# The next chunk's context in four whole rows, loaded into the place of its low part

## What is computed

```python
# x [1,64,512], ctx [1,6272,512]; 32 query heads on 8 key/value heads of 128
q = (layernorm(x) @ Wq + bq)            # 32 heads
k, v = split(ctx @ Wkv + bkv)           # 8 heads each
scores = einsum(q, k) / sqrt(128)
attn = softmax(scores)                  # over all 6272 keys
x = x + (attn @ v) @ Wo + bo
# then: weights are table[codes] * scales (4-bit codes), LoRA parts are added
x = x + attn_and_ffn(layernorm(x))
x = x + linear_with_fourier_update(layernorm(x))
```

## Time and profile before

| | us |
|---|---|
| median of 3 runs | 1094.21 |
| lowest and highest | 1093.18, 1095.26 |
| the profiled execution | 1092.23 |
| its span, first to last instruction | 1090.4 |
| busy in it: PE, DVE, ACT, POOL | 1048.7, 761.8, 586.8, 471.9 |
| idle of PE ahead of `p_kv` matmuls that waited for `v_lo` | 8.5 |
| idle of ACT ahead of `ctx_hi`, waiting for the load of `ctx_st` | 15.5 and 14.5 |
| idle of POOL ahead of `ctx_lo`, waiting for ACT | 25.2 and 24.9 |

### The profile page before, as it was taken

One profiled execution on the slowest core, in us unless ns is written; L12 is line 12 of the kernel. 1 busy time (PEld: TensorE's weight loads), 2 busy tenths in 40 slices (PEclk: granted clock), 3 DMA queues, 4 the chain that ended last, 5 costly groups with the idle time before them and its releaser, 6 DMA issues.

```text
span 1090.4 us, 19501 instructions
## 1 busy us (share of the span) xinstructions
PE 1048.7 (96%) x7035; PEld 959.6 (88%) x7035; DVE 761.8 (70%) x1651; ACT 586.8 (54%) x1233; POOL 471.9 (43%) x633
## 2 busy tenths in 40 slices
PE   6989999999999999999999999999999997999786
PEld 4989999999999999999999999999999996998332
DVE  3447777787777877767877778777777764776663
ACT  2136565566555665556665556655566553665210
POOL 2025454454445454445543454544555433443320
PEclk9689999999999999999999999999999998999988
DMA  9612222122212221121211222212212126435574
GB/s 354 237 48 66 57 66 68 47 75 64 65 53 67 61 66 56 55 70 57 78 63 45 66 71 62 66 39 70 72 57 75 40 63 208 127 112 153 160 233 138
DMA packets 68340, 98.96 MB, mean 91 GB/s; under 512 B 7636, under 2 KB 36820, under 8 KB 67604
## 3 DMA queue, kind: packets, MB, share of 16 engines
q1 hardware_dynamic: 66884, 90.33, 26.9%
q10 hardware_dynamic: 1120, 6.03, 1.4%
q0 software_dynamic: 240, 1.36, 0.3%
HBM read 82.79 MB, written 14.89 MB: 90 GB/s over the span
## 4 chain that ended last, share of the span: by engine, by line
PE 85%; DVE 3%; DMA 2%; SPq 2%; POOL 1%; issue 1%; ACT 0%; POOLq 0%; DVEq 0%
PE p_kv L73 18%; PE p_kv L74 18%; PE p_kv L75 18%; PE p_t L721 8%; PE p_o L73 4%; PE p_o L74 4%; PE p_o L75 4%; PE p_s L774 2%; PE p_s L73 2%; PE p_s L74 2%; PE p_s L75 2%; SPq L511 2%; DMA expanded_weights<-slots 1%; PE p_ot L709 1%; DMA ring_lo<-expanded_weights 1%; DVE probs L1162 1%
## 5 line engine op out<-in xcount | busy, mean ns | idle before, releaser
L603 POOL TENSOR_SCALAR slots<-code 128x512 f32<-128x512 bf16 x232 | 154.2, 665 | 240.3 <-DVE slots L1178 159.0
L1174 DVE TENSOR_TENSOR slots<-slots 128x512 f32<-128x512 f32 x232 | 175.6, 757 | 10.4 <-POOL slots L603 8.4
L1030 ACT ACTIVATE slots<-code,drop_and_offsets 128x512 f32<-128x512 bf16 x232 | 148.4, 714 | 30.7 <-POOL slots L623 30.7
L623 POOL TENSOR_TENSOR slots<-slots 128x512 f32<-128x512 f32 x58 | 75.8, 1307 | 195.9 <-DVE slots L1174 195.9
L1127 DVE TENSOR_TENSOR v_lo<-p_kv,v_hi 128x256 fp32r<-128x256 f32 x196 | 83.1, 424 | 109.2 <-ACT v_hi L997 108.0
L997 ACT ACTIVATE v_hi<-p_kv 128x256 fp32r<-128x256 f32 x196 | 75.2, 384 | 148.2 <-PE p_kv L75 148.0
L997 ACT ACTIVATE k_hi<-p_kv,bk_sb 128x448 fp32r<-128x448 f32 x112 | 71.1, 635 | 154.2 <-PE p_kv L75 153.9
L1129 DVE SCALAR_TENSOR_TENSOR k_lo<-p_kv,bk_sb,k_hi 128x448 fp32r<-128x448 f32 x112 | 76.4, 682 | 108.6 <-ACT k_hi L997 107.6
L1139 DVE TENSOR_TENSOR pt_lo<-p_t,pt_hi 128x512 fp32r<-128x512 f32 x224 | 133.5, 616 | 23.2 <-ACT pt_hi L1008 23.1
L1008 ACT ACTIVATE pt_hi<-p_t 128x512 fp32r<-128x512 f32 x224 | 115.2, 543 | 38.9 <-PE p_t L721 38.9
L73 PE MATMUL p_kv<-wkv_hi,ctx_even_hi 128*128 128x256 f32 x448 | 127.1, 284 | 8.6 <-DVE v_lo L1127 7.7
(11 more groups left out here) (208 smaller groups left out, 2742.7 us busy)
## 6 DMA issues: line engine op xcount, KB each, us to landing
code<-in_codes SPq DMA_DIRECT2D x58, 256.0 KB, 2.6
scale<-in_scales SPq DMA_DIRECT2D x116, 128.0 KB, 3.1
expanded_weights<-slots SPq DMA_DIRECT2D x56, 256.0 KB, 2.0
ctx_st<-in_ctx_t SPq DMA_DIRECT2D x96, 112.0 KB, 2.1
wq_sb<-in_wq SPq DMA_DIRECT2D x8, 1024.0 KB, 13.8
ring_hi<-expanded_weights SPq DMA_DIRECT2D x22, 256.0 KB, 5.5
ring_lo<-expanded_weights SPq DMA_DIRECT2D x22, 256.0 KB, 5.7
stage<-in_wkv ACTq DMA_DIRECT2D x4, 1024.0 KB, 8.6
```

The source lines that it names most:

```text
L603: nc.gpsimd.tensor_scalar(slots[:, slot, :], code16[:], LINES[j][0], LINES[j][1], ALU.mult, ALU.add).then_inc(pool_lines, 1)
L1030: nc.scalar.activation(slots[:, slot, :], code16[:], ACT.Identity, bias=offsets[:, k:k + 1], scale=LINES[j][0]).then_inc(act_lines, 1)
L1174: nc.vector.tensor_tensor(slots[:, slot, :], slots[:, slot, :], slots[:, other, :], ALU.max).then_inc(merged, 1)
```

## The change

The staging place goes. A load now brings one whole row of the next chunk, 128x896, straight to the place of its low part (`ctx_raw` is a second name for `ctx_even_lo` and `ctx_odd_lo`). ScalarE rounds the whole row from there into the high part, and GpSimd subtracts in place: the raw row is overwritten with the low part. So there are four loads, four roundings and four subtractions for a chunk instead of sixteen of each. Loads no longer wait for a subtraction; from the third chunk on, a load waits for the last use of the place by TensorE two chunks earlier. Each row has a semaphore of its own. The rows are spread over the pairs by `PAIR_PIECES = (2, 1, 1, 0)`: two in pair 0, one each in pairs 1 and 2, always the first one in the even block behind value tile 1, and in pair 0 the second one behind the second turned probabilities. A place of the same size as the old staging place stays reserved for the small tensors that lie over it in the later parts.

```diff
--- before.py
+++ after.py
@@ -61,9 +61,8 @@
 GU_TILES = KT * GU_COLS
 NT = ATT_TILES + GU_TILES + FT
 EXTRA = NT - NCH * NKV
-PIECE = CHUNK // 4
-PIECES = KT * (CHUNK // PIECE)
-PAIR_PIECES = (5, 5, 5, 1)
+PIECES = KT
+PAIR_PIECES = (2, 1, 1, 0)
 EPS = 1e-5
 HIGHEST = 3.0e38
 
@@ -307,7 +306,7 @@
 
 
     with ExitStack() as st:
-        ctx_st = sb(st, "ctx_st", [P, PIECE], F32)
+        sb(st, "small_rows", [P, 224], F32)
         ctx_hi = [even_hi, sb(st, "ctx_odd_hi", [P, KT, CHUNK], F32R)]
         ctx_lo = [even_lo, sb(st, "ctx_odd_lo", [P, KT, CHUNK], F32R)]
         v_hi = sb(st, "v_hi", [P, CT, 2 * D], F32R)
@@ -333,7 +332,8 @@
         p_o = psum(st, "p_o", [P, 512])
         p_ot = psum(st, "p_ot", [P, 512])
 
-        ctx_in, ctx_rounded, ctx_split = sem("ctx_in"), sem("ctx_rounded"), sem("ctx_split")
+        ctx_in = [sem(f"ctx_in{k}") for k in range(KT)]
+        ctx_rounded, ctx_split = sem("ctx_rounded"), sem("ctx_split")
         kv_psum, kv_rounded, kv_split = sem("kv_psum"), sem("kv_rounded"), sem("kv_split")
         scores_psum, scores_out = sem("scores_psum"), sem("scores_out")
         stat_step, max_ready = sem("stat_step"), sem("max_ready")
@@ -388,6 +388,7 @@
 
             return nc.alloc_sbuf_tensor_at(name, shape, F32, offset=where[place] + skip)
 
+        ctx_raw = [over("ctx_even_raw", [P, KT, CHUNK], "ctx_even_lo"), over("ctx_odd_raw", [P, KT, CHUNK], "ctx_odd_lo")]
         ring_odd = over("ring_odd", [P, RING_ODD, 2, TW], "ctx_odd_hi")
         extra = over("extra_tiles", [P, EXTRA, TW], "ctx_odd_hi", RING_ODD * 2 * TW * 4)
         ring_hi = over("ring_hi", [P, KT, 2 * NKV * D], "wkv_hi")
@@ -416,7 +417,7 @@
         bb_sb, lb_d, w_four, z2t = place_in_turn("probs", (
             ("bb_sb", row), ("lb_d", [RANK, HID]), ("w_four", [RR, HID]), ("z2t", turned_rows)))
         e_small, = place_in_turn("o_t", (("e_small", [RANK, 4, TOK]),))
-        stats, mv, spare = place_in_turn("ctx_st", (
+        stats, mv, spare = place_in_turn("small_rows", (
             ("stats", [TOK, 2, 6]), ("mv", [TOK, 2, 4]), ("spare", [P, 8])))
 
         pb = [p_kv[:, 0], p_kv[:, 1], p_s[:, 0], p_s[:, 1], p_t[:, 0], p_t[:, 1], p_o[:], p_ot[:]]
@@ -480,10 +481,9 @@
         def _(sp):
             def load_ctx(s, piece, first=False):
 
-                if not first:
-                    sp.wait_ge(ctx_split, PIECES * (s - 1) + piece)
-                k, q = piece // 4, piece % 4
-                sp.dma_start(ctx_st[:], ctx_t[s, k, :, q * PIECE:(q + 1) * PIECE]).then_inc(ctx_in, 16)
+                if s >= 2:
+                    sp.wait_ge(kv_psum, k_use(s - 2, NKV - 2, 1) + 1)
+                sp.dma_start(ctx_raw[s % 2][:, piece], ctx_t[s, piece]).then_inc(ctx_in[piece], 16)
 
             def codes_of(n, first=False):
                 if not first:
@@ -585,11 +585,9 @@
         def _(pool):
             def split_ctx(s, piece, half):
 
-                n, k = PIECES * (s - 1) + piece, piece // 4
-                keys = slice(piece % 4 * PIECE, (piece % 4 + 1) * PIECE)
-                wait_apart(pool, ctx_rounded, n + 1, pool_passed)
-                nc.gpsimd.tensor_tensor(ctx_lo[half][:, k, keys], ctx_st[:], ctx_hi[half][:, k, keys].bitcast(F32),
-                                        ALU.subtract).then_inc(ctx_split, 1)
+                wait_apart(pool, ctx_rounded, PIECES * (s - 1) + piece + 1, pool_passed)
+                nc.gpsimd.tensor_tensor(ctx_lo[half][:, piece], ctx_raw[half][:, piece],
+                                        ctx_hi[half][:, piece].bitcast(F32), ALU.subtract).then_inc(ctx_split, 1)
 
             def narrow(n, first=False):
                 wait_apart(pool, code_in, 16 * (n + 1), pool_passed)
@@ -1017,9 +1015,9 @@
                 if last or q >= PAIR_PIECES[h // 2]:
                     return
                 piece = sum(PAIR_PIECES[:h // 2]) + q
-                act.wait_ge(ctx_in, 16 * (PIECES * s + piece + 1))
-                keys = slice(piece % 4 * PIECE, (piece % 4 + 1) * PIECE)
-                nc.scalar.activation(ctx_hi[1 - par][:, piece // 4, keys], ctx_st[:], ACT.Copy).then_inc(ctx_rounded, 1)
+                act.wait_ge(ctx_in[piece], 16 * (s + 1))
+                nc.scalar.activation(ctx_hi[1 - par][:, piece], ctx_raw[1 - par][:, piece], ACT.Copy).then_inc(
+                    ctx_rounded, 1)
 
             def lines(n, first=False):
```

## The result

The changed kernel takes 1113.52 us (median of 4 runs, 1111.93 to 1115.45) against 1093.7 for the kernel before (4 runs, 1093.09 to 1095.26). The ratio is 1.0172, with a 95% interval of 1.0138 to 1.0207: slower by 19.8 us, where 18.3 was forecast (1112.5, range 1102 to 1122). The profiled execution of the changed kernel is the slowest of its four, 1115.45, with a span of 1113.5.

What follows compares the result with a forecast made beforehand. TensorE was taken as the bound, so what counts is whether `v_lo` comes in time. Late tiles -1.5 and 18 places x 1.1 = 19.8 sum to +18.3 us on the median 1094.2: 1112.5 us, range 1102 to 1122.

Steps and rivals of the forecast that it cites:

- Late tiles: Two value tiles start late on TensorE behind a late GpSimd subtraction; loads no longer wait for it: -1.5 us.
- Step 1, the load: Even blocks, 18 places: row load issued at 238.0, lands 3.3 us later, up to 4 allowed; 4.2 still costs nothing.
- the prediction's own sign: Load or rounding is wrong if ScalarE waits for the row by more than about 0.5 us.
- The rival of the late row: Row lands 4.7 us after issue instead of 4.2, sliding rounding and subtraction by 0.5: 9 us more, 1121.5; chance 0.10.
- Step 2, the rounding: ScalarE between value tiles 1 and 2: 0.94 us in 0.93 free, no cost if the row landed.
- Step 3, the subtraction: GpSimd behind the CAST: 128x896 takes 2.13 us, upper bound 2.67.
- Step 4, the merge: VectorE's merge 2 waits for GpSimd's whole instruction and ends 0.55 us behind its end, at 245.93.
- Step 5: `v_lo` of tile 3 late, so TensorE starts value tile 5 late: 1.1 us in each of 18 places, 19.8.
- What lies behind merge 2: Value tile 6 keeps its room; second row of pair 0 costs 0; pair 3, nothing loaded, 0.
- The sum: Late tiles -1.5 plus 19.8 for the 18 places: +18.3 us.

Runs made afterwards that it cites:

- e4: Changed kernel with one row in each pair, rounding moved behind the even block's second turned probabilities, subtraction behind the table lines: 1090.59 us, ratio 0.9973.
- e6: Changed kernel with each pair's first row loaded in the pair before and each subtraction in four 128x224 instructions: 1089.23 us, ratio 0.9929.
- e1: Changed kernel with each row's subtraction on GpSimd in four 128x224 instructions at the same place: 1096.54 us, ratio 1.0037.
- e2: Changed kernel with the whole-row subtraction moved behind the table lines, where VectorE's inputs are in PSUM: 1096.75 us, ratio 1.0028.
- e7: Changed kernel with GpSimd filling the row with zeros, reading nothing, instead of subtracting: 1096.26 us, one run.
- e3: Changed kernel with each pair's first row loaded in the pair before, for pair 0 in the chunk before: 1110.82 us, ratio 1.0169.
- e9: The kernel of e4 run again with more rounds, against the kernel before: 1092.52 us, ratio 1.0005.

## Why the prediction was right

- *Late tiles, -1.5.* Both went; in e4 and e6, with nothing else in the way, no late tile is left and the stretch is 1.9 us shorter (two more tiles, at 410 and 677 us, had been late by 0.2 to 0.3).
- *Step 1, the load: 3.3 us expected, up to 4 allowed.* Too low. The median is 3.9, the longest 5.2, and a row's rounding never began less than 3.75 after issue in the 17 places behind the first. The step counted on issue at 238.0 in each place; in three places the two issues of scales took 1.9 to 2.4 us instead of 1.1, so the row was issued late, in three others it landed 4.3 to 5.2 after issue. Those are the six late tiles 4, 5.3 us in the profiled execution. ScalarE waited for its row by 0.5 to 1.6 us in seven places, so by the prediction's own sign this step was wrong there. The rival of the late row (chance 0.10) thus took place in a third of the places, beside the forecast and not instead of it.
- *Step 2, the rounding: 0.94 expected, 0.953 measured*, hidden as said (e6).
- *Step 3, the subtraction: 2.13 expected, 2.12 measured.* The line through 224 and 512 elements held at 896.
- *Step 4, the merge.* It ended 0.54 to 0.56 behind the end of GpSimd's instruction in all 18 places, as behind 0.66 and 0.84 before. e1, e2 and e7 tell its conditions: one instruction's length, VectorE at a merge, GpSimd reading. e1 shows the other order too: a subtraction that starts within a merge takes 1.11 to 1.14 us instead of 0.66. The Trainium skill's rule (SBUF — State Buffer, "SBUF: two separate sides") says the same; it had promised the whole length, and the trace now shows it at 2.12.
- *Step 5, 1.08 to 1.1 a place, 19.8 in all.* Measured 18.8 in the changed kernel and 19.8 in e3; by the stretch 19.6, from the changed kernel to e1 and again from e3 to e6. Two thirds of the difference lie in the six places where a late row had already shifted the tiles.
- *What lies behind merge 2.* No tile 6 was late, the second row of pair 0 cost nothing, pair 3 neither.
- *The sum.* 18.3 forecast, 19.8 measured in the medians, with 15 to 23 by the interval. By the stretch the change costs 22.5: 19.6 for the long subtraction, 4.8 for late rows, less 1.9. So the main term and its cause were right, and the late rows, put at nothing, are the term that was missing. That the medians came within 1.5 us of the forecast owes something to luck: they lie 3 us under the two profiled executions' difference.

## What to carry to other kernels

Before making one long instruction of several short ones on GpSimd, look at what VectorE does beside it: here an instruction of VectorE with two inputs in SBUF waited for the *end* of a GpSimd instruction that reads SBUF and began first, and ended 0.55 us behind it, so its length, not its rate, is the price. Compare that length with the room of whoever waits for VectorE, here about 0.4 us. And where the bound engine waits once for 7 us (8.8 with the lower granted clock behind it), removing that is worth more than 144 instructions saved on engines that aren't the bound.

## What the runs showed that I had not expected

The wait of some 7 us in the last chunk was a matter of order on one queue: a store of 256 KB behind twenty loads of weights. Moving it ahead gave 9 us against e4's median and 11 against e9's, where 7 were expected; the traces place 8.8: the wait, and the granted clock that had fallen during it. It is the largest gain against the kernel before, and no arithmetic changed for it. And splitting GpSimd's work in four made it slower by itself, 3.45 us against 2.12, and the kernel faster by 15 (ratios) to 17 us (medians).
